# An expert loop in which the down product moves between the gate half and the up half of a slot

## The reference, cut to what matters

```python
logits = x @ router_w + router_b                 # top 4 of 16 experts per token
gu   = einsum('th,ehf->tef', x, gate_up_proj) + gate_up_bias
gate = minimum(gu[..., ::2], LIMIT)
up   = clip(gu[..., 1::2], -LIMIT, LIMIT)
glu  = gate * sigmoid(gate * ALPHA)
act  = (up + 1.0) * glu
out  = einsum('te,teh->th', scores, einsum('tei,eih->teh', act, down_proj) + down_bias)
```

## Time and profile before

| | |
|---|---|
| time, median of 3 runs | 728.5 us (726.91 to 730.75) |
| the profiled execution | 725.6 us, its span 723.8 us |
| PE busy | 620.2 us, 86% of the span |
| VectorE busy | 491.5 us, 68% |
| ACT busy | 540.3 us, 75% |
| POOL busy | 282.6 us, 39% |

### The profile page before, as it was taken

How to read it: one execution, slowest core, us unless ns; L and a number is a source line. 1 busy time by engine, 2 the same in 40 slices (tenths; PEclk the granted TensorE clock), 3 DMA queues, 4 the chain that set the end, 5 groups by cost and what they waited for, 6 DMA issues and landing times.

```text
span 723.8 us, 11190 instructions
## 1 busy us (share of the span) xinstructions
PE 620.2 (86%) x3623; PEld 363.7 (50%) x3623; DVE 491.5 (68%) x1277; ACT 540.3 (75%) x745; POOL 282.6 (39%) x307
## 2 busy tenths in 40 slices
PE   2898998979999899999997599888887988889667
PEld 2576666657776667677675223232322322323244
DVE  3889888879988899899898344355542454634343
ACT  4665656666867767577475599899999999999622
POOL 3277467676766766474656212031400010000010
PEclk9999999999999999999999599999999999999955
DMA  9100432322333323243322994000079700000001
GB/s 242 54 1 1 133 102 89 102 81 95 105 99 92 89 92 111 92 118 115 105 88 46 185 199 154 1 1 1 1 133 190 145 1 1 1 1 15 17 2 29
DMA packets 32382, 56.64 MB, mean 78 GB/s; under 512 B 4752, under 2 KB 13424, under 8 KB 30944
## 3 DMA queue, kind: packets, MB, share of 16 engines
q1 hardware_dynamic: 31136, 55.48, 29.3%
q0 software_dynamic: 224, 0.34, 0.2%
q10 hardware_dynamic: 960, 0.07, 0.1%
HBM read 35.72 MB, written 3.38 MB: 54 GB/s over the span
## 4 chain that ended last, share of the span: by engine, by line
PE 30%; issue 20%; ACT 20%; DVE 15%; POOL 12%; DMA 1%; ACTq 1%; DVEq 0%; POOLq 0%
ACT raw_w L1070 14%; POOL act_parts L796 8%; PE bank L2139 7%; PE bank L1811 4%; PE bank L1813 3%; PE bank L1812 3%; PE bank L2107 3%; DVE act L1354 3%; DVE bank L1343 2%; DVE up L1332 2%; POOL rstd L743 2%; DVE stats L1192 1%; PE bank L1965 1%; DMA vecs<-in_vecs 1%; PE bank L1962 1%
## 5 line engine op out<-in xcount | busy, mean ns | idle before, releaser
L1070 ACT ACTIVATE raw_w<-bank,minus_c 128x1024 f32<-128x1024 f32 x256 | 259.7, 1155 | 10.6 <-PE bank L2107 9.8
L796 POOL TENSOR_TENSOR act_parts<-act,act_parts 128x512 fp32r<-128x512 f32 x128 | 167.7, 1313 | 104.7 <-ACT act_parts L996 102.9
L996 ACT ACTIVATE act_parts<-act 128x512 fp32r<-128x512 f32 x128 | 80.7, 631 | 98.4 <-DVE act L1354 98.2
L1650 DVE TENSOR_TENSOR bank<-bank,fix 128x256 f32<-128x256 f32 x128 | 55.2, 431 | 123.5 <-PE bank L2107 123.1
L1811 PE MATMUL bank<-xn_parts,w_hi 128*128 128x512 f32 x256 | 109.4, 428 | 12.4 <-DVE up L1332 9.8
L1332 DVE TENSOR_SCALAR up<-bank,b_up 128x512 f32<-128x512 f32 x128 | 95.3, 745 | 24.3 <-PE bank L1813 22.2
L1813 PE MATMUL bank<-xn_parts,w_hi 128*128 128x512 f32 x256 | 101.4, 396 | 0.0
L1812 PE MATMUL bank<-xn_parts,w_lo 128*128 128x512 f32 x256 | 101.2, 395 | 0.0
L1354 DVE SCALAR_TENSOR_TENSOR act<-up,bank 128x512 f32<-128x512 f32 x128 | 86.7, 677 | 0.0
L982 ACT ACTIVATE bank<-bank,b_gate 128x512 f32<-128x512 f32 x112 | 73.0, 652 | 10.4 <-PE bank L1813 10.1
L2139 PE MATMUL bank<-raw_w,act 128*9 128x512 f32 x512 | 66.9, 595 | 15.0 <-ACT raw_w L1070 14.8
(11 more groups left out here) (252 smaller groups left out, 985.8 us busy)
## 6 DMA issues: line engine op xcount, KB each, us to landing
grow<-scores SPq DMA_DIRECT2D x48, 256.0 KB, 3.1
early<-scores SPq DMA_DIRECT2D x32, 256.0 KB, 3.2
raw_w<-scores SPq DMA_DIRECT2D x32, 256.0 KB, 3.1
raw_w<-in_gate_up SPq DMA_DIRECT2D x4, 512.0 KB, 8.7
w_lo<-gelu_parts SPq DMA_DIRECT2D x8, 256.0 KB, 5.3
w_lo<-act_parts SPq DMA_DIRECT2D x8, 256.0 KB, 5.5
w_hi<-gelu_parts SPq DMA_DIRECT2D x6, 256.0 KB, 4.6
w_hi<-act_parts SPq DMA_DIRECT2D x6, 256.0 KB, 5.7
```

What stands on the lines that cost most here:

```text
L796: pool.tensor_tensor(act_lo[:, j % NACT, :], act[:, j % NACT, :], act_hi[:, j % NACT, :].bitcast(F32), ALU.subtract).then_inc(s["lo_ready" ...
L996: eng.activation(act_hi[:, j % NACT, :], act[:, j % NACT, :], ACT.Copy).then_inc(s["hi_ready"], 1)
L1070: eng.activation(probs[:, u % NP, :], pair, ACT.Exp, bias=minus_c[:, b:b + 1])\
```

## The change

On PE the function of the two halves is cut in two, and the loop calls gate half, down product of three slots back, up half, score. On VectorE expert_act of the last slot stands ahead of expert_up of this one. No instruction, wait, tile or transfer is added or dropped; the order on ACT, POOL and SP is as it was.

```diff
             for slot in range(FIRST_SLOT, JOBS + 3):
+                if 1 <= slot <= JOBS:
+                    expert_act(slot - 1)
                 if 0 <= slot < JOBS:
                     expert_up(slot)
-                if 1 <= slot <= JOBS:
-                    expert_act(slot - 1)
                 if slot > E0 and slot % E0 == 2:
                     add_out(slot // E0 - 1)
...
-            def expert_halves(j):
+            def expert_gate_half(j):
...
+            def expert_up_half(j):
+                e, c, f = j % E0, j // E0 % NC, j // E0 // NC
+                at = chunk(c)
                 if j >= 1:
                     pe.wait_ge(s["up_ready"], j)
...
                 if 0 < slot < JOBS:
-                    expert_halves(slot)
+                    expert_gate_half(slot)
+                if slot >= 3:
+                    expert_down(slot - 3)
+                if 0 < slot < JOBS:
+                    expert_up_half(slot)
                 if 0 <= slot < JOBS:
                     expert_score(slot)
-                if slot >= 3:
-                    expert_down(slot - 3)
```

More of the change, by code:

```diff
@@ L2293, in _ @@
                 if slot == EARLY_SLOT:
-                    expert_halves(0)
+                    expert_gate_half(0)
+                    expert_up_half(0)
                 if slot == 0:
```

## The result

The changed kernel takes 743.7 us (median of 4 runs, 743.04 to 751.04) where the kernel before takes 728.4 in the same rounds: ratio 1.0252, 95% interval 1.0207 to 1.0298. It is slower, as forecast, but by 15.3 us instead of 5.4, and outside the range. The profiled execution took 744.0 us, its span is 742.2.

A forecast was written before the change was run, and what follows sets the result against it. It took PE and VectorE as both close to their limit, with PE setting plain slots. Terms 4.1 + 2.0 + 3.5 - 2.2 - 2.0 = +5.4 us on the median of 728.5 gave 733.9 us, range 727.0 to 738.5.

The forecast's parts named there:

- six chunk ends: PE waits for add_out before the bias product, the up half no longer filling that wait: 6 x 0.69 = 4.1 us lost.
- low parts behind a norm: Five places where POOL's norm delays the low part; the up half now follows PE's wait: 5 x 0.69 = 3.5 us lost.
- late statistics: Norm statistics on VectorE come later at or behind chunk ends: 0.9 us at slot 67, 1.1 at three others, 2.0 lost.
- state space chains: Four chains beginning with act, which comes 0.66 us earlier and pulls them forward: 4 x 0.55 = 2.2 us gained.
- routing exps: Places where ACT's gelu and table loads wait for act; act 0.66 us earlier gains 0.5 us at each of four.
- first gelu: The single wait for gelu in the first chunk (1.5 us), led by act, counted within 4 x 0.5 = 2.0 us gained.
- The price of zero: In a plain slot, without side work, the shifts on PE and VectorE cancel, so the change costs nothing there.
- the term 6 x 0.69: Loss at six of seven chunk ends, each costing PE a full third of a slot, 0.69 us: 4.1 us.
- The rival "no change": Low parts starting 0.66 us earlier run less beside the scan, saving 3.3 in four chains: 730.6 or 728.6 us; chance 0.25.
- The worse rival: The gains fail because something other than act holds ACT's next step; the losses stay: 738.1 us; chance 0.13.
- the symmetry on which the plain slot's price rests: In plain slots act, high and low part come 0.66 us earlier and PE asks for them 0.69 earlier: price zero.

The follow-up runs named there:

- VectorE's half alone: The changed kernel with TensorE's loop put back as before, so only act ahead of up on VectorE remains: 728.2 us, ratio 1.0003.
- without VectorE's half: The changed kernel with VectorE's lines back in their old order, so only TensorE's new order remains: 772.6 us, ratio 1.0615.

## Why the prediction was right and wrong

The start of each gate half, after less before, shows where the loop's 19.9 us arose:

| place | forecast, us | measured, us |
|---|---|---|
| six chunk ends (slots 19, 35, 67, 83, 99, 115) | 4.1 | 9.0 |
| low parts behind a norm (13, 22, 37, 53, 69), with late statistics | 3.5 + 2.0 | 6.4 |
| state space chains (28 to 81) | -2.2 | +1.0 |
| routing exps and first gelu | -2.0 | -0.5 |
| places without a price (15 to 17: 2.0; 72: 0.9; others) | 0 | 4.0 |

**Plain slots: right.** Between the places of the table the shift mostly changes by 0.00 to 0.03 us a slot. The price of zero held.

**Chunk ends: the mechanism right, the term mis-sized.** At the three ends without a fall of the clock (35, 83, 115) the shift is 0.78, 0.59 and 0.78 us, on average 0.72 where 0.69 was forecast. At 19, 67 and 99 it is 2.36, 2.17 and 2.37. The difference, some 4.7 us, is the up half and what follows at half clock. The step that failed here is the term 6 x 0.69: the added idle time, 0.96 us at slot 67, was priced by its length alone, and the matmuls behind it were taken at the full clock of the earlier trace rows; no term stood for a fall.

**Low parts and late statistics: right in sum.** 1.03, 0.78, 1.40, 1.31 and 0.92 us make 5.4 against 5.5 (the late statistics add up to 0.9 + 1.2 = 2.1, not 2.0); behind slot 37 the clock takes another 0.9. Together the four falls at places that were foreseen cost about 5.7 us, which agrees with the 4.7 us found by filling and with the 1.5 us that one fall cost between two executions of one kernel. The fifth fall lies in the 2.0 us of slots 15 to 17. The clock was 1.00 all through the loop of before; I read that row as a state of things, where it was that of one execution with short gaps, the longest 1.7 us.

**State space chains: wrong sign.** The step that failed is that act, 0.66 us earlier, pulls the whole chain forward. It did bring the low part ahead of the scan, but then it was the scan that was slow. Before (second chain; start, length):

```profile
148.05 1.28 DVE L1382 TENSOR_TENSOR_SCAN raw_w<-raw_w,zero 128x512 f32<-128x512 f32 x1
148.28 2.11 POOL L796 TENSOR_TENSOR act_parts<-act,act_parts 128x512 fp32r<-128x512 f32 x1 [0.31 <-ACT act_parts L996]
```

and after:

```profile
154.75 1.30 POOL L796 TENSOR_TENSOR act_parts<-act,act_parts 128x512 fp32r<-128x512 f32 x1
155.09 2.02 DVE L1382 TENSOR_TENSOR_SCAN raw_w<-raw_w,zero 128x512 f32<-128x512 f32 x1
```

Whichever starts second is stretched, here by 0.7 to 0.8 us. Before it was the low part, which has slack of its own; now it is the scan, which holds up VectorE. The rival "no change" had counted on a quicker low part and got it (1.30 for 2.07), at the scan's cost. The Trainium skill ("GPSIMD Engine Reference", Key points) names the contention of GpSimd with VectorE instructions that have two SBUF inputs; the trace agrees (2.02 us for 1.28), and adds that VectorE can be the one that pays. VectorE's half alone has the long scans too, and in the same slots (28 to 34, 43 to 49, 57 to 65, 75 to 81) it loses 1.4 us where the changed kernel loses 1.0. So the sign of this term is set by VectorE's order and not by TensorE's; that kernel's time stays the same because it gains elsewhere (it waits 3.8 us for low parts in place of 9.0). That the scans are the whole cause of the lost 3.2 us was not tried separately.

**Routing exps: half right.** At slots 9 to 10 and 122 to 127 0.5 and 0.7 us were gained, as forecast; at 105 to 111 only 0.15, and at 93 to 96 0.9 were lost. There a small VectorE instruction on the routing shares (L1278), 0.18 us before, takes 1.03 us behind a low part that had started 0.32 us ahead of it; with VectorE's half alone it takes 1.04, and the same slots lose as much. It was not tried separately either.

**Places without a price.** At slot 15 VectorE comes late to up behind the long scan of the state space's powers (3.2 us). TensorE used to fill a part of that time with the down product at the end of the slot before; now that product is done sooner, and the up half had an idle 2.88 us where it had 1.59. At slot 72 TensorE's transposes of the routing shares now wait 0.67 us for VectorE, and did not before. It is the same meeting as at the scan, at an instruction that had 0.21 us. Before, then after:

```profile
230.10 0.21 DVE L1278 SCALAR_TENSOR_TENSOR share_hl<-picked,recip 128x64 f32<-128x64 f32 x1
```

```profile
242.97 1.28 POOL L796 TENSOR_TENSOR act_parts<-act,act_parts 128x512 fp32r<-128x512 f32 x1 [2.16 <-ACT act_parts L996]
243.02 1.31 DVE L1278 SCALAR_TENSOR_TENSOR share_hl<-picked,recip 128x64 f32<-128x64 f32 x1
```

The first was in the trace of before, among the waits for VectorE's up, and I gave it no price.

**The whole.** The losses that I did price came to 9.6 us, and without the clock they measured 9.7. The sum failed by what was added to them: the clock (5.7), gains that did not come (4.7: 4.2 forecast, a loss of 0.5 measured), and unpriced places (4.0). The worse rival had the gains failing, with 0.13 and for another reason (ACT's rows), but no rival had the clock. And the symmetry on which the plain slot's price rests, product forward by 0.66 and demand forward by 0.69, hid how much the one covers the other: without VectorE's half TensorE's costs 45 us, not a few.

## What to carry to other kernels

Before a consumer is moved forward in its engine's order, look up by how much its operands are early at the slots with side work, not at the plain ones; where there is no slack, one more buffer of distance can be worth more than the order (here a gain of 4 us over before in three of four orders, against a loss of 15). Price a new gap on TensorE by its length and by the matmuls that may follow at half clock (here some 1.5 us a fall). Look, too, at which VectorE instructions a new order puts beside the GpSimd work. And when two halves of a change feed each other, try each alone: here one was worth nothing and the other cost 45 us.

## What the runs showed of the hardware

- The granted clock fell to 1.2 GHz for some 3.4 us behind stalls of TensorE of 0.96 to 2.9 us, in a loop that otherwise had 1.00. The length of the stall alone does not decide: stalls of 2.05 us at 97.6 and of 2.37 us at 189.8 in the changed kernel were not followed by a fall, one of 0.96 at 228.3 was. Nor does the kernel decide: behind the same stall (2.95 and 2.93 us) in two executions of one kernel the clock stayed up once and fell once, at a cost of 1.5 us. Filling the eight longest stalls with matmuls took the falls in the loop from five to two.
- A scan on VectorE and a subtraction on GpSimd that overlap do not share evenly: the first keeps its own pace (1.28 and 1.30 us above), the second is stretched (2.11 and 2.02). In all 52 such meetings in the kept traces the second ends 1.06 to 1.09 us after the first, whether it began 0.03 or 0.54 us behind it. In all runs with up first the scans average 1.25 us, in all with the product first 1.93 us or more.
- Small VectorE instructions are stretched too: one on the routing shares took 1.31 us behind a low part that began 0.05 us before it, and 0.21 without one.
